# One kernel of token mixing and a quantised layer: the per-step order of all five engines rewritten

## The chip, the core and the metric

One core of one Trainium2 chip. The metric is the device time of one execution in microseconds, here the median of 3 runs; lower is better.

## The reference, cut to what matters

```python
x = x + attn(layernorm(x))            # x: (2, 4096, 512) f32
x = x + ffn(layernorm(x))
# attn, per token: mix = x + xx*time_maa_x;  lo = tanh(mix @ maa_w1.T) @ maa_w2  (4 branches)
#   xm = x + xx*(lo + time_maa)  ->  r, k, v, decay w, gates a, ma, mk, output gate g
# then per head (32 x 32 state s), token after token:
sa = einsum('bhij,bhj->bhi', s, a_)
s = s*w_ + sa*b_ + v_*k_
y = einsum('bhij,bhj->bhi', s, q_)
# y: group norm per head, affine, + bonus, * g, @ Wo.T
# ffn: per row x_q = round(x/x_scale), x_q @ weight_q.T, * x_scale*weight_scale + bias
```

## The kernel before, in words

The 4096 tokens of both sequences are cut into 64 tiles of 64 tokens, so a tile has 128 rows. The recurrence is solved in chunks of 32 tokens (two chunks, c = 0 and 1, in a tile) for 16 heads: within a chunk it is a triangular system, whose inverse is made by squaring (`power` 0, 1, 2, then `half_inverse` and `inverse`), and only the 32 x 32 state passes from chunk to chunk.

The work is a pipeline over tiles. One call of `tile_step(i)` on each engine does four things for four different tiles: **mix** for tile j = i+1 (layer norm, transpose, the four mixed inputs), **project** for tile i (keys, queries, values, gates), **solve** for tile m = i-1 (scores, powers, inverse, the two chunks) and **finish** for tile n = i-2 (group norm, output projection `project_out`, residual, quantisation, `feed_forward`). There are 62 or so full steps, a few partial ones at both ends. The instructions are straight-line code, with no loop on the chip.

Every engine (TensorE `pe`, VectorE `dve`, ScalarE `act`, GpSimd `pool`, SyncE `sp` for the loads and stores) has its own `tile_step`, and the calls in it are the order in which that engine works, written out by hand. Each engine works strictly in that order; between engines there are counting semaphores only: `p_...` is counted up by TensorE, `v_...` by VectorE, `a_...` by ScalarE, `g_...` by GpSimd. A helper such as `quantised(n)` on TensorE waits for `v_q2` (the rows quantised by VectorE), for `v_xm` (VectorE has read the bank that the transpose will overwrite) and then does four transposes.

The names that matter here:
- TensorE: `scores_b`, `scores_k` (64 matmuls each, L1186), `gates` (L1151), `power` (128 matmuls of 32*32, L1208), `half_inverse` (128, L1216), `inverse` (128, L1224), `from_values` (32, L1236), `from_state` (32, L1243), `solve_step` (64, L1252), `from_solutions` (32, L1262), `project_out` (2 matmuls a block, L1272), `transposed_input` (L1103), `low_rank`, `gate_hidden`, `hidden`, `keys`, `queries`, `values` (8 matmuls a block, L1069), `decay_gate`, `output_gate` (L1076), `mixed_inputs` (L1122), `quantised` (L1281), `feed_forward` (L1288). In all 1316 matmuls a step, each with a weight load of its own.
- VectorE: `shift_mix` (xx, then mix, L769), `undecayed` (bt L819, kt L822), `residual` (xres, then its statistics), `update_state` (L900), `decayed_state` (s_old), `quantiser`, `quantised_rows`, `mixed_inputs` (xm_wa and three more, L779), `right_hand_sides` (L896), `decayed` (the two products that make aq).
- ScalarE: `front_transposed` copies the transposed tile to xT; an ACT_TABLE_LOAD is put before a function whose table is not loaded.
- GpSimd: `undecayed` (kmod, kkp, kmod again), `bonus`, `bonus_values` (qkT from rk), `norm2_rstd`, `residual_bias` (x2b), `finish_rows`, `mixed_inputs` (four adds).

## Time and profile before

| | us |
|---|---|
| median of 3 runs | 3234.86 |
| lowest and highest run | 3229.97, 3236.03 |
| profiled execution, span from first to last instruction | 3230.6 |
| TensorE matmuls busy | 3026.2 (94%) |
| TensorE weight loads busy | 2676.0 (83%) |
| VectorE busy | 2659.6 (82%) |
| ScalarE busy | 1987.8 (62%) |
| GpSimd busy | 1252.0 (39%) |
| mean granted clock of TensorE | 0.991 |

Busy time is the union of an engine's instructions; a matmul's end is modelled, so TensorE at 94% is not TensorE at its peak. "issue" in a chain or as releaser is time in which the engine waited for nothing that the profile shows. The profiled execution has no separate time of its own beside its span of 3230.6 us; it lies within the three runs (3229.97 to 3236.03 us).

### The profile page before, as it was taken

To read this page: it belongs to the slowest core of one execution; us is meant where nothing else is said; L and a number is where in the kernel's file an instruction comes from. 1 tells how busy PE (TensorE), PEld (TensorE's weight loads), DVE (VectorE), ACT (ScalarE), POOL (GpSimd) and SP (SyncE) were. 2 spreads that over 40 slices of the span, in tenths; PEclk is the share of its full clock that TensorE was granted. 3 is DMA by queue.
4 is the path that set the end of the run, shared out by engine and by line. 5 is a ranking of instruction groups with operands and counts; after the bars stand their busy time and mean duration, and the time that the engine had idled before them with its cause. 6 is when DMAs were issued, how large, how long until landed. Compare 5 with 4: busy or idle time off the path is not lost.

```text
span 3230.6 us, 182735 instructions
## 1 busy us (share of the span) xinstructions
PE 3026.2 (94%) x84224; PEld 2676.0 (83%) x84224; DVE 2659.6 (82%) x5443; ACT 1987.8 (62%) x3519; POOL 1252.0 (39%) x1161
## 2 busy tenths in 40 slices
PE   5899999999999999999999999999999999999996
PEld 5888888888888888888888888888888888888884
DVE  4687888888888888887888888888888888888885
ACT  3575665665765756756666657567566566566563
POOL 4234334334344344343343343433433433434332
PEclk9999999999999999999999999999999999999998
DMA  3000000000000000000000000000000000000000
GB/s 119 10 23 15 22 20 16 23 20 17 23 20 17 23 20 17 23 20 17 20 18 22 20 17 23 20 17 23 20 17 23 18 18 20 18 22 20 17 17 19
DMA packets 39380, 70.47 MB, mean 22 GB/s; under 512 B 9812, under 2 KB 10836, under 8 KB 38616
## 3 DMA queue, kind: packets, MB, share of 16 engines
q1 hardware_dynamic: 38616, 58.77, 6.7%
q8 instruction: 664, 10.88, 1.4%
q14 instruction: 100, 0.82, 0.1%
HBM read 41.97 MB, written 16.78 MB: 18 GB/s over the span
## 4 chain that ended last, share of the span: by engine, by line
PE 93%; issue 5%; DVE 1%; SPq 1%; ACT 1%; DMA 0%; POOL 0%; POOLq 0%; ACTq 0%; DVEq 0%
PE bank L1069 30%; PE bank_a L1208 12%; PE bank L1272 8%; PE bank_a L1186 4%; PE bank L1076 4%; PE bank_b L1186 4%; PE bank_b L1243 3%; PE bank_b L1236 3%; PE bank_a L1236 3%; PE bank_a L1243 3%; PE bank_a L1216 2%; PE bank_a L1224 2%; PE bank_b L1262 2%; PE bank L1151 2%; PE bank_a L1262 2%
## 5 line engine op out<-in xcount | busy, mean ns | idle before, releaser
L504 ACT ACT_TABLE_LOAD x383 | 491.4, 1283 | 19.3 <-DVE shift L761 12.5
L1069 PE MATMUL bank<-xm_rg,w_r 128*128 128x128 f32 x2048 | 285.4, 282 | 3.5 <-issue 2.7
L1272 PE MATMUL bank<-w_o,yc 128*128 128x512 f32 x512 | 270.8, 630 | 11.1 <-DVE yc L744 9.3
L1208 PE MATMUL bank_a<-pw,w_ffn_int 32*32 32x64 f32 x16384 | 262.0, 215 | 20.1 <-issue 14.9
L1069 PEld LDWEIGHTS bank<-xm_rg,w_r 128*128 128x128 f32 x2048 | 248.9, 191 | 27.9 <-issue 16.9
L1208 PEld LDWEIGHTS bank_a<-pw,w_ffn_int 32*32 32x32 f32 x16384 | 237.4, 105 | 39.4 <-issue 19.0
L1069 PEld LDWEIGHTS bank<-xm_k,w_k 128*128 128x128 f32 x2048 | 241.4, 194 | 12.4 <-issue 3.3
L1069 PE MATMUL bank<-xm_v,w_v 128*128 128x128 f32 x2048 | 249.9, 275 | 1.7 <-DVE kk L744 1.7
L1069 PE MATMUL bank<-xm_k,w_k 128*128 128x128 f32 x2048 | 242.0, 277 | 3.2 <-issue 3.0
L1069 PEld LDWEIGHTS bank<-xm_v,w_v 128*128 128x128 f32 x2048 | 239.2, 192 | 1.8 <-issue 1.8
L504 ACT ACTIVATE u<-bank_b,parity 128x256 f32<-128x256 f32 x128 | 53.7, 470 | 290.8 <-PE bank_b L1252 290.8
L870 DVE STREAM_TRANSPOSE w_ffn_int<-bank_a 128x512 f32<-128x512 f32 x192 | 137.4, 716 | 94.7 <-ACT pw L504 94.4
L399 POOL TENSOR_TENSOR yc<-yc,rkv 128x512 f32<-128x512 f32 x64 | 82.0, 1281 | 327.3 <-ACT yc L504 327.3
L504 ACT ACTIVATE u<-bank_a,parity 128x256 f32<-128x256 f32 x128 | 53.7, 470 | 242.2 <-PE bank_a L1252 242.2
L399 POOL TENSOR_TENSOR xm_wa<-xm_wa,xT 128x512 f32<-128x512 f32 x64 | 75.3, 1177 | 327.9 <-DVE xm_wa L779 327.9
L396 POOL TENSOR_TENSOR kept<-ga,gma 128x512 f32<-128x512 f32 x64 | 81.6, 1274 | 287.1 <-ACT ga L504 287.1
L396 POOL TENSOR_TENSOR kkp<-kk,pinv 128x512 f32<-128x512 f32 x64 | 75.3, 1176 | 288.5 <-DVE kk L744 288.5
L396 POOL TENSOR_TENSOR kmod<-kraw,pinv 128x512 f32<-128x512 f32 x64 | 77.6, 1213 | 258.8 <-ACT pinv L504 258.8
L1208 PE MATMUL bank_a<-first,w_ffn_int 32*32 32x64 f32 x8192 | 134.9, 215 | 26.2 <-issue 25.3
L399 POOL TENSOR_TENSOR o_sb<-o_sb,x2b 128x512 f32<-128x512 f32 x64 | 81.7, 1276 | 200.5 <-DVE o_sb L968 200.5
L396 POOL TENSOR_TENSOR qkT<-qkT,faaaa_T 128x512 f32<-128x512 f32 x64 | 81.5, 1273 | 166.5 <-DVE qkT L914 166.5
L744 DVE TENSOR_TENSOR first<-bank_a,mask_b 128x1024 f32<-128x1024 f32 x64 | 78.4, 1225 | 81.6 <-PE bank_a L1186 81.6
(204 smaller groups left out, 8579.9 us busy)
## 6 DMA issues: line engine op xcount, KB each, us to landing
xin<-in_x SPq DMA_DIRECT2D x128, 128.0 KB, 2.7
xres<-in_x SPq DMA_DIRECT2D x128, 128.0 KB
out<-o_sb SPq DMA_DIRECT2D x128, 128.0 KB, 2.5
w_ffn_int<-in_weight_q SPq DMA_DIRECT2D x1, 2048.0 KB, 9.7
w_k<-in_Wk SPq DMA_DIRECT2D x1, 1024.0 KB
w_r<-in_Wr SPq DMA_DIRECT2D x1, 1024.0 KB
w_v<-in_Wv SPq DMA_DIRECT2D x1, 1024.0 KB
w_o<-in_Wo SPq DMA_DIRECT2D x1, 1024.0 KB, 14.9
```

What stands on the lines that cost most here:

```text
L396: return nc.gpsimd.tensor_tensor(out_, in0, in1, ALU.mult)
L399: return nc.gpsimd.tensor_tensor(out_, in0, in1, ALU.add)
L504: return nc.scalar.activation(out_, in_, func, **kw)
L870: V.transpose(pt, pairs(bank_a)[:, :, 0, :]).then_inc(v_ptT, 1)
L1069: ins = mm(bank[:, o * n:(o + 1) * n], weights[:, k, o * P:(o + 1) * P], x[:, k].rearrange("p b t -> p (b t)"), start=(k == 0), stop=(k == ...
L1076: ins = mm(bank[:, o * TOK:(o + 1) * TOK], weights[:, o * P:(o + 1) * P], hidden[:], start=True, stop=True)
L1186: ins = mm(bank[q, 64 * n:64 * n + 64], both(keys_[q, g]), both(aq[q, g, 0:2]), start=True, stop=True)
L1208: ins = mm(bank_a[q, 64 * n:64 * n + 64], pt[q, g, :], source[q, g, 0:2].rearrange("p j t -> p (j t)"), start=True, stop=True)
L1236: mm(bank[q, 4 * CHUNK * j:4 * CHUNK * j + 3 * CHUNK], both(vT2[q, g]), km[q, g].rearrange("p j t -> p (j t)"), start=(j % 4 == 0), stop=F ...
L1243: ins = mm(bank[q, 4 * CHUNK * j:4 * CHUNK * j + 3 * CHUNK], both(s_old2[q, j]), aq[q, g].rearrange("p j t -> p (j t)"), start=False, stop ...
L1262: ins = mm(bank[q, 4 * CHUNK * j + CHUNK:4 * CHUNK * j + 3 * CHUNK], both(u2[q, j]), first[q, g, 2:4].rearrange("p j t -> p (j t)"), start ...
L1272: ins = mm(fb[0][:], yc[:, k * TOK:(k + 1) * TOK], w_o[:, k, :], start=(k == 0), stop=(k == KB - 1))
```

## The change

The same operations on the same operands. On each engine but SyncE the calls in `tile_step` come in a new order. Three waits are written out that the old order gave by itself (GpSimd `bonus` for `v_k`, GpSimd `residual_bias` for `v_x2`, VectorE `undecayed` for `g_qk`). ScalarE loads its tables by name, four times in a full step.

```diff
@@ -424,6 +424,7 @@
 
             def bonus(m):
                 pool.wait_ge(v_q, count(m, 1, 1))
+                pool.wait_ge(v_k, count(m, 1, 1))
                 mul(qk, aq[:, :, 1, :], kt[:]).then_inc(g_qk, 1)
 
             def weighted_bonus(m):
@@ -451,6 +452,7 @@
                 nc.gpsimd.tensor_tensor(rs2[:, 1:2], rs2[:, 0:1], minus_half[:], ALU.pow).then_inc(g_rs2, 1)
 
             def residual_bias(n):
+                pool.wait_ge(v_x2, count(n, 1, 1))
                 add(x2b[:], xres[:], ffn_bias[:]).then_inc(g_x2b, 1)
 
             def finish_rows(n):
@@ -460,27 +462,26 @@
 
             def tile_step(i, mix=True, project=True, solve=True, finish=True):
                 j, m, n = i + 1, i - 1, i - 2
+                if solve:
+                    bonus(m)
+                    decayed_state(m)
                 if mix:
                     norm_rstd(j)
+                if solve:
+                    weighted_bonus(m)
+                if finish:
+                    add_bonus(n)
                 if project:
                     kept_keys(i)
-                if solve:
-                    decayed_state(m)
-                    bonus(m)
-                if finish:
-                    add_bonus(n)
-                if solve:
-                    weighted_bonus(m)
-                if project:
                     undecayed(i)
+                if finish:
+                    norm2_rstd(n)
                 if solve:
                     bonus_values(m)
-                if finish:
-                    norm2_rstd(n)
+                if mix:
+                    mixed_inputs(j, XWA, XRG)
+                if finish:
                     residual_bias(n)
-                if mix:
-                    mixed_inputs(j, XWA, XRG)
-                if finish:
                     finish_rows(n)
 
             constants()
@@ -639,8 +640,10 @@
                 act.wait_ge(v_ysqT, count(n, 1, 0))
                 run(ysq[:], y_sb[:], ACT.Square).then_inc(a_ysq, 1)
 
-            def exp_tables():
-                nc.scalar.preload_act_table_set("natural_log_exp_and_others")
+            EXP_LN, SIGMOID_TANH = "natural_log_exp_and_others", "sigmoid_and_others"
+
+            def tables(functions):
+                nc.scalar.preload_act_table_set(functions)
 
             def log_variance(n):
                 act.wait_ge(v_yvar, count(n, 1, 1))
@@ -666,62 +669,65 @@
                 j, m, n = i + 1, i - 1, i - 2
                 if solve:
                     removal_pairs(m)
+                if project:
+                    keys(i)
+                if solve:
                     key_pairs(m)
-                if project:
-                    keys(i)
-                if finish:
-                    squared_heads(n)
                 if project:
                     ma_gate(i)
                     a_gate(i)
+                if finish:
+                    squared_heads(n)
+                    tables(EXP_LN)
+                    log_variance(n)
+                if solve:
+                    power(m, 0)
+                if project:
+                    tables(SIGMOID_TANH)
+                    mk_gate(i)
                     squares(i)
-                    mk_gate(i)
-                if solve:
-                    power(m, 0)
-                if finish:
-                    log_variance(n)
+                    decay_gate(i)
+                if finish:
+                    tables(EXP_LN)
                     inverse_deviation(n)
-                if project:
-                    decay_gate(i)
                 if solve:
                     power(m, 1)
+                    value_pairs(m)
+                if project:
+                    log_squares(i)
+                    log_sigmoid(i)
+                    values(i)
                 if finish:
                     head_affine(n)
                 if solve:
-                    value_pairs(m)
-                if project:
-                    log_sigmoid(i)
+                    power(m, 2)
+                if project:
+                    exponentials(i)
+                    key_decay(i)
                 if mix:
                     normalised(j)
-                if solve:
-                    power(m, 2)
-                if project:
-                    values(i)
+                if project:
+                    queries(i)
                 if mix:
                     front_transposed(j)
-                if project:
-                    log_squares(i)
-                    exp_tables()
-                    key_decay(i)
-                    exponentials(i)
+                if solve:
+                    solution(m, 0)
+                if project:
+                    tables(SIGMOID_TANH)
+                    gate_hidden(i)
                 if mix:
                     low_rank(j)
-                if project:
-                    queries(i)
-                if solve:
-                    solution(m, 0)
+                if solve:
                     output_gate(m)
-                if project:
-                    gate_hidden(i)
+                if finish:
+                    quantised(n)
                 if solve:
                     solution(m, 1)
-                if finish:
-                    quantised(n)
+                    outputs(m, 0)
                 if mix:
                     hidden(j, 0)
                     hidden(j, 1)
                 if solve:
-                    outputs(m, 0)
                     outputs(m, 1)
 
             act.wait_ge(const_done, 1)
@@ -819,6 +825,7 @@
                 V.scalar_tensor_tensor(bt[:], by_chunk(ga), -1.0, kkp[:], ALU.add, ALU.mult).then_inc(v_b, 1)
                 dve.wait_ge(g_keep, count(i, 1, 1))
                 dve.wait_ge(g_kz, count(i, 1, 1))
+                dve.wait_ge(g_qk, count(i, 1, 0))
                 V.scalar_tensor_tensor(kt[:], by_chunk(kept), -1.0, kmod[:], ALU.add, ALU.mult).then_inc(v_k, 1)
 
             def decayed(i):
@@ -973,45 +980,46 @@
                 if mix:
                     norm_input(j)
                 if solve:
+                    token_major_values(m)
                     scores_b(m)
+                    enter(m)
                 if finish:
                     head_variance(n)
                 if project:
                     removal_keys(i)
                 if solve:
-                    token_major_values(m)
-                    enter(m)
                     power(m, 0)
+                    token_major_keys(m)
                 if project:
                     key_norm(i)
+                if solve:
+                    scores_k(m)
+                    bonus_rows(m)
+                    power(m, 1)
+                if finish:
+                    head_norm(n)
+                if project:
+                    key_decay(i)
+                if solve:
+                    bonus_sums(m)
+                    power(m, 2)
+                    right_hand_sides(m, 0)
+                if project:
+                    decay_sums(i)
+                if finish:
+                    gate_heads(n)
                 if mix:
                     norm_shift(j)
                 if solve:
-                    token_major_keys(m)
-                if finish:
-                    head_norm(n)
-                if solve:
-                    power(m, 1)
-                    scores_k(m)
-                if finish:
-                    gate_heads(n)
-                if project:
-                    decay_sums(i)
-                if solve:
-                    bonus_rows(m)
-                    power(m, 2)
-                if project:
-                    key_decay(i)
+                    half_inverse(m)
+                if project:
+                    removal_directions(i)
+                if solve:
+                    inverse(m)
                 if mix:
                     shift_mix(j)
-                if solve:
-                    half_inverse(m)
-                    inverse(m)
-                if project:
-                    removal_directions(i)
-                if solve:
-                    right_hand_sides(m, 0)
-                    bonus_sums(m)
+                if project:
+                    undecayed(i)
                 if finish:
                     residual(n)
                 if solve:
@@ -1019,19 +1027,17 @@
                     decayed_state(m)
                 if finish:
                     quantiser(n)
+                    quantised_rows(n)
+                if mix:
+                    mixed_inputs(j, XWA, XWA)
                 if solve:
                     right_hand_sides(m, 1)
-                if finish:
-                    quantised_rows(n)
-                if mix:
-                    mixed_inputs(j, XWA, XWA)
+                if mix:
                     mixed_inputs(j, XK, XV)
                 if solve:
                     bonus(m)
                 if mix:
                     mixed_inputs(j, XRG, XRG)
-                if project:
-                    undecayed(i)
                 if solve:
                     update_state(m, 1)
                 if project:
@@ -1295,66 +1301,68 @@
                     keys(i, [2, 3])
                 if solve:
                     scores_b(m)
+                if project:
+                    gates(i)
+                if solve:
                     scores_k(m)
-                if project:
-                    gates(i)
-                if solve:
                     power(m, 0)
                 if project:
                     queries(i, [0])
+                    decay_gate(i)
                     values(i, [0])
-                    decay_gate(i)
                 if solve:
                     power(m, 1)
                 if project:
-                    queries(i, [1])
                     values(i, [1])
                     values(i, [2])
                     values(i, [3])
-                    queries(i, [2])
+                    queries(i, [1])
                 if solve:
                     power(m, 2)
                     from_values(m, 0)
+                    from_state(m, 0)
+                    half_inverse(m)
+                if project:
+                    queries(i, [2])
+                    queries(i, [3])
+                if finish:
+                    project_out(n, [0])
+                    project_out(n, [1])
+                if solve:
+                    inverse(m)
                 if mix:
                     transposed_input(j)
-                if project:
-                    queries(i, [3])
-                if finish:
-                    project_out(n, [0])
-                if solve:
-                    half_inverse(m)
-                if finish:
-                    project_out(n, [1])
+                if finish:
                     project_out(n, [2])
+                if solve:
+                    solve_step(m, 0)
+                if finish:
+                    project_out(n, [3])
+                if solve:
+                    output_gate(m)
+                    from_solutions(m, 0)
+                if project:
+                    gate_hidden(i)
                 if mix:
                     low_rank(j)
                 if solve:
-                    inverse(m)
-                    from_state(m, 0)
-                if finish:
-                    project_out(n, [3])
-                if solve:
-                    solve_step(m, 0)
-                if project:
-                    gate_hidden(i)
-                if solve:
-                    from_solutions(m, 0)
-                    output_gate(m)
                     from_values(m, 1)
+                if mix:
+                    mixed_inputs(j)
+                if solve:
                     from_state(m, 1)
-                if mix:
-                    mixed_inputs(j)
+                if finish:
+                    quantised(n)
                 if solve:
                     solve_step(m, 1)
                 if finish:
-                    quantised(n)
+                    feed_forward(n)
+                if mix:
+                    hidden(j, 0)
                 if solve:
                     from_solutions(m, 1)
                 if mix:
-                    hidden(j, 0)
                     hidden(j, 1)
-                if finish:
-                    feed_forward(n)
 
             pe.wait_ge(const_done, 1)
             pe.wait_ge(mix_loaded, MIX_LOADED)
```

## Rows read from the trace of the kernel before

**Rows 1.** Windows: 60 full steps; one undisturbed step; one with stalls

```profile
core 0: us, PE busy (x) PEld busy (x) DVE busy (x) ACT busy (x) POOL busy (x), PEclk, DMA share, GB/s
119.80:3070.70 2950.90, 2820.41 (x78962) 2497.42 (x78963) 2487.66 (x5100) 1864.34 (x3301) 1157.23 (x1019) 1.00 0.07 20
...
1743.42:1791.15 47.73, 46.83 (x1316) 41.52 (x1316) 41.74 (x86) 30.98 (x56) 19.27 (x17) 1.00 0.08 20
1546.40:1596.65 50.25, 47.11 (x1316) 41.59 (x1317) 41.44 (x86) 31.19 (x56) 19.27 (x17) 1.00 0.08 20
```

**Rows 2.** Chain that ended last, step from 1743 us: start, us, what

```profile
1763.90 0.59 PE bank L1103 x4
...
1766.24 1.22 PE bank_a L1216 x82
1767.46 1.91 PE bank L1272 x4
...
1770.26 1.19 PE bank_a L1224 x86
...
1773.98 0.68 PE bank_b L1252 x50
...
1775.75 1.09 PE bank_b L1262 x32
1776.84 1.09 PE bank L1076 x8
1777.92 1.47 PE bank_a L1236 x32
1779.39 1.32 PE bank_a L1243 x32
1780.71 1.10 PE bank L1122 x32
...
1782.50 0.68 issue
```

**Rows 3.** Timeline of TensorE, step from 1546 us (pauses inside a group)

```profile
1551.37 1.98 PE L1208 MATMUL bank_a<-first,w_ffn_int 32*32 32x64 f32 x127
1554.52 0.21 PE L1208 MATMUL bank_a<-first,w_ffn_int 32*32 32x64 f32 x1 [1.17 <-issue]
...
1576.85 1.53 PE L1243 MATMUL bank_b<-aq,s_old 64*64 64x96 f32 x31 [0.47 <-issue]
```

**Rows 4.** DMA queues, the page: kind, packets, MB, share of 16 engines

```profile
q8 instruction: 664, 10.88, 1.4%
```

**Rows 5.** Timeline of ScalarE, the copy to xT

```profile
1764.59 0.60 ACT L504 ACTIVATE xT<-bank 128x512 f32<-128x512 f32 x1 [0.70 <-PE bank L1103]
```

**Rows 6.** Timeline of VectorE, the same step

```profile
1765.93 0.69 DVE L744 TENSOR_TENSOR xx<-xT 128x512 f32<-128x512 f32 x1
1766.66 1.14 DVE L769 SCALAR_TENSOR_TENSOR mix<-xx,maa_x,xT 128x128 f32<-128x128 f32 x4
...
1774.13 0.68 DVE L744 TENSOR_TENSOR xres<-bank,xres 128x512 f32<-128x512 f32 x1
...
1776.87 0.45 DVE L900 STREAM_TRANSPOSE state<-bank_b 128x256 f32<-128x256 f32 x1 [0.93 <-PE bank_b L1262]
1777.36 1.74 DVE L744 TENSOR_TENSOR s_old<-state,plast 128x512 f32<-128x512 f32 x1
...
1780.76 0.45 DVE L896 STREAM_TRANSPOSE rhs_sb<-bank_a 128x256 f32<-128x256 f32 x1
...
1781.95 1.12 DVE L779 SCALAR_TENSOR_TENSOR xm_wa<-bank,maa,xx 128x128 f32<-128x128 f32 x4
```

**Rows 7.** The tile kt: VectorE's product, ns min/median/max

```profile
L822 DVE SCALAR_TENSOR_TENSOR kt<-kept,kmod x64: 679/1672/1675, 58.4 to 3159.4; 128x512 f32<-128x512 f32 x64
```

**Rows 8.** Timeline of GpSimd, the same step

```profile
1775.73 1.05 POOL L396 TENSOR_TENSOR qkT<-w_ffn_int,rk 128x512 f32<-128x512 f32 x1
...
1777.25 1.30 POOL L399 TENSOR_TENSOR x2b<-xres,ffn_bias 128x512 f32<-128x512 f32 x1
```

**Rows 9.** Costliest groups, the page: ScalarE's table loads

```profile
L504 ACT ACT_TABLE_LOAD x383 | 491.4, 1283 | 19.3 <-DVE shift L761 12.5
```

20 lines of the change are left out of this document (10 added, 10 removed).

## The prediction

> **What bounds the kernel now.** I read the windows first, for the length of a step and who fills it. Sixty full steps take 2950.9 us, 49.18 us each, and TensorE's matmuls are busy in 2820.4 us of them (96%); VectorE in 84%, ScalarE in 63%, GpSimd in 39% [rows 1]. TensorE's granted clock is 1.00 there, the upper of its two levels (2.4 GHz), and it never pauses long enough to lose it, so the clock is no term. Then the chain that ended last, for what stands between the matmuls. In a step of 47.73 us it is matmuls end to end, and only one pause repeats in step after step: 0.68 us of "issue" in front of `quantised` [rows 2]. `quantised` waits for `v_q2` and for `v_xm`, the second because VectorE must have read bank 1 before the transposes overwrite it; the last part of xm_wa ends at 1781.95 + 1.12 = 1783.07, and the pause at 1782.50 + 0.68 = 1783.18 [rows 2, 6]. So that pause is VectorE being late.
>
> The third view is TensorE's timeline in a longer step (50.25 us with the same 1316 matmuls [rows 1]). There a `power` group of 128 matmuls runs 127, stands still for 1.17 us, and runs the last one; a `from_state` group pauses for 0.47 us in the same way [rows 3]. Nothing in the kernel waits inside a group. The instruction queue shows what it is: 664 packets, 10.88 MB, so 16.4 kB each [rows 4]. TensorE has 2 x 84224 instructions, or 254 a packet: each packet is a block of about 256 instructions, 128 matmuls with their weight loads. The 127 matmuls took from 1551.37 to 1553.35 and the 128th came at 1554.52, so I take it that a block cannot be begun sooner than about 3.2 us after the one before (1554.52 - 1551.37 = 3.15). A `power` group eats one in 2.0 us. A step has 2632 such instructions, 10.3 blocks, so the boundaries wander over the groups and steps differ. The mean step is 49.18 - 47.73 = 1.45 us above the good one, and that one still has a short pause: these stalls cost some 1.5 to 2 us a step. The Trainium skill ("Runtime: NRT & Kernel Launch", Instruction fetch mechanics) says that the refill is 16 KiB blocks of 256 instructions, which the packets agree with, and that fetch is hidden because issue is slower than the fill; by that rule the stall would be nought, and the trace has 1.17 us.
>
> **What TensorE itself gains.** The groups are the same, so its matmul time stays. Tile shapes change about as often as before: `gates` now stands between `scores_b` and `scores_k`, but `from_values` and `from_state` stand together, and so do `gate_hidden` and `low_rank`. I put that at 0, ends -0.2 and +0.2 us a step (a group of 8 matmuls at a change, 1.09 us in `output_gate` [rows 2], carries about 0.2 of it).
>
> **The pause before `quantised`.** In the new order it comes behind `mixed_inputs` and `from_state(1)`, still with both waits. I measure both ways from the start T of `transposed_input`.
> TensorE: `transposed_input` 0.59, block 2 of `project_out` 0.96 (half of 1.91), `solve_step` 0.68, block 3 0.96, `output_gate` 1.09, `from_solutions` 1.09, `gate_hidden` and `low_rank` 2 x 1.09 less the 0.2 of one change, `from_values` 1.47, `mixed_inputs` 1.10, `from_state` 1.32 [rows 2]: 11.2 us.
> VectorE: the copy to xT ends 1.29 after T (1764.59 + 0.60 - 1763.90) [rows 2, 5]; xx and mix 0.69 + 1.14 [rows 6]; bt and kt, which now stand here, 0.68 each if nothing blocks them [rows 7]; then xres to the end of xm_wa. That stretch lasts 1783.07 - 1774.13 = 8.94 before; less the idle 0.93 and the rhs_sb of 0.45 that now comes after, 7.56 [rows 6]. Sum 12.04, and two handoffs of about 0.1: 12.2 us.
> So TensorE waits about 1.0 us where it waited 0.68: **+0.3**.
>
> The uncertain part of the 7.56 is one blocked instruction. kt takes 679 ns once and 1672 at the median, with a GpSimd add beside it [rows 7]; s_old took 1.74 beside x2b [rows 6, 8]. Its unblocked price I estimate from kt's 0.68 (same size, two SBUF inputs), so the block is 1.06. In the new order x2b is later, but `bonus_values` (1.05) starts just when s_old or x2n does, since it is queued behind `norm2_rstd` [rows 8]. I keep one block. Ends: none, and the wait is gone (12.2 - 1.06 is under 11.2), -0.68; a second one, xx behind the last kmod product, +0.5 more, +0.8 in all. The Trainium skill ("SBUF — State Buffer", SBUF: two separate sides) says that VectorE with two SBUF inputs and GpSimd hold a shared port pair exclusively for a whole instruction; the kt row agrees, and it speaks against an order that lays them side by side.
>
> **Behind it.** `feed_forward` now comes after `solve_step(1)`, 1.0 us behind the start of `quantised`; ScalarE must copy qT (0.60 like xT [rows 5]) after the transposes: +0.1. `solve_step(1)` finds its rhs_sb just ready. `hidden(0)` needs GpSimd's add to xm_wa, 1.2 us later, and has 1.9. `keys` has about 0.8 us to spare.
>
> **Instruction blocks.** Before, `power(2)` to `half_inverse` is 2.4 blocks in 7.1 us (2.0 for the power group [rows 3], 1.47, 0.59, some 0.9 for a block of queries, 0.96, 1.22) and `inverse` to `solve_step(0)` 1.8 blocks in 4.3 (1.19, 1.47, 0.96, 0.68) [rows 2]. At 3.2 a block they lack 0.5 and 1.4. After, `power(2)`, `from_values`, `from_state`, `half_inverse` stand together: 2.5 blocks in 6.1, lacking 1.9. `inverse` to `solve_step(0)` lacks 1.5, but that lies after T, where VectorE sets the end and the wait swallows it. So exposed 1.9 before and 1.9 after; I take **+0.1**, with ends -0.3 and +0.6, since how boundaries fall is averaged here.
>
> **ScalarE and the rest.** Six loads a step become four, 2 x 1.283 = 2.6 us less of an engine 63% busy [rows 1, 9]. No pause of TensorE was put down to it: 0. What it would cost if that cover went: a_pw, gate and the u copies have 0.6 to 1 us each before TensorE needs them in the new order. The added waits: `bonus` for `v_k` stands behind `v_q`, which VectorE does later still; `undecayed` for `g_qk` of a tile earlier, long done; `residual_bias` for `v_x2` is issued after the adds, later than the residual. Each 0; behind the last stands `finish_rows`, which needs `v_ffn` later anyway. Loads and stores keep their order, and xres is needed 30 us into a step.
>
> **Sum.** +0.3 +0.1 +0.1 = +0.5 us a step, over 62 steps +31 us. Against the execution's 3230.6 that is 3262; the median of the runs lies 4.3 above it, so **3266 us**.
>
> **Rivals.**
> A, faster: `bonus_values` slips clear of s_old and x2n, VectorE reaches xm_wa by T + 11.2, and the pause of 0.68 goes. That is -0.68 + 0.1 = -0.6 a step, -36: 3199. It decides on one GpSimd instruction of 1.05 us. For it: VectorE's sum without a block is 11.1. Against: nothing else moves that instruction.
> B, a draw: the wait stays what it was, one pause for another: 3235.
> C, much slower: VectorE has no idle time from xx to the next `power(0)`. At the step's end both products of aq now meet GpSimd's xm_rg add and x2b, two blocks of up to 1 us, then vT meets `bonus`; ptT for `power(0)` comes at about the moment TensorE wants it. A microsecond late, or block stalls at their upper end (+0.6), give +1.5 a step: 3328.
> D, the change doesn't do what it says: the table loads stay six. ScalarE has the room; the time is the forecast's.
>
> **How the numbers follow.** The forecast (with D) 0.44, rival A 0.30, B 0.13, C 0.13. The forecast's own ends (wait +0.1 to +0.8, blocks -0.3 to +0.6) go from 3240 to 3300. The range of 8 in 10 takes in A and the lower half of C: 3196 to 3308. A measurement tells 0.2%, 6.5 us or 0.1 us a step, from no change. Faster 0.30, same 0.13, slower 0.57.
>
> **What would show it.** In the changed kernel's chain: about 1 us of "issue" before L1281; s_old or x2n over 1.4 us beside GpSimd's qkT; pauses within the `half_inverse` group, fewer in L1243; four ACT_TABLE_LOADs a step; good steps near 48.0. Wrong would be: no pause before L1281 (A), or a new pause before the first L1208 group or L1186 (C).

## The result and the profile after

The changed kernel takes 3260.99 us (median of 4 runs, 3258.61 to 3263.92), the kernel before 3235.45 on the same chip (4 runs, 3229.97 to 3238.58): a ratio of 1.0081 [1.0067, 1.0096]. The profiled execution spans 3259.1 us, at a mean granted clock of 0.985 (before: 0.991).

The page of the changed kernel: span, engines, the queue that brings instructions, ScalarE's table loads.

```profile
span 3259.1 us, 182613 instructions
...
PE 3046.3 (93%) x84224; PEld 2689.4 (83%) x84224; DVE 2720.8 (83%) x5443; ACT 1756.2 (54%) x3334; POOL 1275.2 (39%) x1161
...
q8 instruction: 664, 10.88, 1.4%
...
L646 ACT ACT_TABLE_LOAD x256 | 328.4, 1283 | 4.6
```

ScalarE's other group of table loads, after and then before:

```profile
L505 ACT ACT_TABLE_LOAD x6 | 7.7, 1283 | 12.3 <-DVE shift L767 12.2
```

```profile
L643 ACT ACT_TABLE_LOAD x64 | 82.1, 1283 | 1.1
```

The same 84224 matmuls and the same 664 blocks of instructions [rows 4]. The table loads are 262 where they were 447: before, the 64 loads by name come on top of the 383 of [rows 9]. That is 4 a step in place of 7, and ScalarE fell from 62% to 54% busy. The time rose all the same. The windows, with the columns of [rows 1], over the same stretch and in one good step:

```profile
119.80:3070.70 2950.90, 2813.01 (x78513) 2486.74 (x78508) 2523.91 (x5051) 1628.03 (x3099) 1168.29 (x1011) 0.99 0.07 20
...
1747.43:1796.20 48.77, 46.90 (x1318) 41.43 (x1316) 42.78 (x87) 27.12 (x52) 19.70 (x17) 1.00 0.08 20
```

In the same 2950.9 us TensorE did 78513 matmuls where it had done 78962 [rows 1], 0.57% fewer. Its chain shows two kinds of pause (start, us, what):

```profile
1748.48 0.45 issue
1748.93 0.38 PE bank L1287 x4
...
1775.20 0.39 PE bank_b L1242 x5
1775.59 0.62 issue
...
1778.90 0.72 PE bank_a L1222 x52
1779.62 0.16 issue
1779.78 0.71 PE bank_a L1222 x46
...
1786.82 0.48 PE bank_b L1258 x38
1787.31 0.63 issue
1787.93 0.39 PE bank_b L1258 x21
```

The first stands before `quantised`, now L1287, and is 0.45 us where it was 0.68 [rows 2]. The others lie within a group, as in [rows 3]: in `from_values`, in `half_inverse`, in `solve_step(0)`. In both kernels a step has 2656 instructions of TensorE, waits included. I cut each of the 61 full steps of both traces into its groups, by counting weight loads, took the time from the first weight load of a group to that of the next, and subtracted the group's own shortest (5th percentile). For the two waits at the step's end I took the time over 0.68, 1.47 and 0.40 us, what their groups take elsewhere. Without these two, the excess is 2.1 us a step before and 2.8 after:

| excess, mean us a step | before | after |
|---|---|---|
| the three `power` | 0.52, 0.28, 0.05 | 0.37, 0.39, 0.14 |
| `half_inverse` | 0.26 | 0.69 |
| queries behind it | - | 0.27 |
| `inverse` | 0.24 | 0.19 |
| `from_state(0)` | 0.34 | 0.05 |
| `solve_step(0)` | 0.09 | 0.38 |
| the rest | 0.32 | 0.37 |
| pause before `quantised` | 0.72 | 0.30 |
| wait for rhs_sb at `solve_step(1)` | - | 0.11 |
| whole step | 49.15 | 49.55 |

The step is 0.40 us longer; times 61 steps that is 24 us, and 25.5 lie between the medians of the runs. Inside the small-tile groups there are 105 pauses of 0.3 us or more before and 116 after, between one weight load and the next. Counted in instructions from the trace's first one, all of them lie at the same place modulo 256, to one instruction; TensorE's 169984 instructions are 664 x 256, one packet for each block. And each of these pauses, in both traces, ends 1.1 to 1.6 us after a packet of the instruction queue has landed. So the in-group pauses are TensorE waiting for its next block.

A part of the excess is not pause but clock. TensorE's granted clock, 0.99 over the whole stretch by the windows, is 0.50, the lower of its two levels (1.2 GHz), in ten short stretches of the full steps after, 38 us together, and in three before, 10 us. All come behind pauses: in nine of the ten one of 1.7 to 2.3 us, in the tenth one of 1.0. Here is one such stretch, and TensorE's timeline ahead of it and in it, after:

```profile
1085.38:1088.79 3.41, 3.41 (x12) 2.38 (x12) 2.33 (x4) 0.70 (x2) 0.97 (x1) 0.50 0.29 77
```

```profile
1083.96 0.44 PE L1222 MATMUL bank_a<-pw,w_ffn_int 32*32 32x32 f32 x28 [1.69 <-issue]
1084.33 2.85 PE L1075 MATMUL bank<-xm_rg,w_r 128*128 128x128 f32 x16
1086.97 2.79 PE L1278 MATMUL bank<-w_o,yc 128*128 128x512 f32 x4
```

In the step from 1747 us the same two groups take 2.05 and 1.88 us. TensorE is busy while the clock is low, so about half of that time is lost, an estimate: 5 us before and 19 after, 0.1 and 0.3 us a step. The row "queries behind it" is mostly that. The median step is even shorter than before, 49.03 us against 49.41; the mean is longer by the few steps with a long pause and a low clock behind it.

The waits (engine line waited for: us in total, times, longest) from 1000 to 2000 us, after, then before, show it in `half_inverse` (L1222; before, L1216) and before `quantised` (L1287; L1281):

```profile
PE bank_a L1222 <- issue: 10.2, 10, 2.3
PE bank L1287 <- issue: 6.1, 13, 0.7
```

```profile
PE bank L1281 <- issue: 12.9, 19, 0.7
...
PE bank_a L1216 <- issue: 3.6, 5, 1.1
```

VectorE's timeline ahead of the end of xm_wa in one step (T, the start of `transposed_input`, is 1785.38), and GpSimd's beside it:

```profile
1786.69 0.69 DVE L750 TENSOR_TENSOR xx<-xT 128x512 f32<-128x512 f32 x1 [0.83 <-ACT xT L505]
...
1791.89 0.69 DVE L750 TENSOR_TENSOR s_old<-state,plast 128x512 f32<-128x512 f32 x1
1792.50 1.27 DVE L959 TENSOR_SCALAR x2n<-xres,mv,rs 128x512 f32<-128x512 f32 x1
...
1795.97 1.13 DVE L785 SCALAR_TENSOR_TENSOR xm_wa<-bank,maa,xx 128x128 f32<-128x128 f32 x4
```

```profile
1791.58 0.55 POOL L452 TENSOR_TENSOR rs<-rs,minus_half 128x1 f32<-128x1 f32 x1 [4.75 <-DVE rs L955]
1792.09 1.40 POOL L396 TENSOR_TENSOR qkT<-w_ffn_int,rk 128x512 f32<-128x512 f32 x1
```

And the three tiles over the whole run (ns, minimum, median, maximum):

```profile
L750 DVE TENSOR_TENSOR s_old<-state,plast x64: 691/691/1556, 103.3 to 3218.8; 128x512 f32<-128x512 f32 x64
```

```profile
L959 DVE TENSOR_SCALAR x2n<-xres,mv,rs x64: 533/1271/1518, 154.2 to 3246.8; 128x512 f32<-128x512 f32 x64
```

```profile
L829 DVE SCALAR_TENSOR_TENSOR kt<-kept,kmod x64: 679/685/689, 51.9 to 3171.0; 128x512 f32<-128x512 f32 x64
```

kt and s_old run free now, against 1672 ns at the median [rows 7] and 1740 in the step shown [rows 6]. x2n is the one that is blocked, beside qkT, which `norm2_rstd` released 0.4 us earlier.

### The profile page after: what moved, and what is told of

Same layout as the page of the kernel before. It is cut to its first block, busy times and chain, and to the rows that moved or that the text cites. A ratio compares the mean times of both kernels' runs of the same rounds, so it can differ in the third digit from the quotient of the medians.

```text
span 3259.1 us, 182613 instructions
## 1 busy us (share of the span) xinstructions
PE 3046.3 (93%) x84224; PEld 2689.4 (83%) x84224; DVE 2720.8 (83%) x5443; ACT 1756.2 (54%) x3334; POOL 1275.2 (39%) x1161
## 4 chain that ended last, share of the span: by engine, by line
PE 93%; issue 5%; DVE 1%; ACT 1%; POOL 0%; POOLq 0%; ACTq 0%; DVEq 0%
PE bank L1075 30%; PE bank_a L1214 12%; PE bank L1278 7%; PE bank_a L1192 4%; PE bank_b L1192 4%; PE bank L1082 4%; PE bank_b L1242 3%; PE bank_a L1249 3%; PE bank_a L1242 3%; PE bank_b L1249 3%; PE bank_a L1222 3%; PE bank_a L1230 2%; PE bank L1128 2%; PE bank L1157 2%; PE bank_a L1268 2%
## 5 line engine op out<-in xcount | busy, mean ns | idle before, releaser
L1075 PE MATMUL bank<-xm_v,w_v 128*128 128x128 f32 x2048 | 258.2, 279 | 2.8 <-issue 2.8
L505 ACT ACTIVATE qT<-bank 128x512 bf16<-128x512 bf16 x64 | 38.2, 597 | 264.0 <-PE bank L1287 264.0
L452 POOL TENSOR_TENSOR rs<-rs,minus_half 128x1 f32<-128x1 f32 x64 | 35.0, 548 | 354.2 <-DVE rs L955 354.2
L505 ACT ACTIVATE pw<-bank_a 128x512 f32<-128x512 f32 x192 | 113.4, 590 | 103.7 <-PE bank_a L1214 103.7
L505 ACT ACTIVATE pinv<-cum 128x512 f32<-128x512 f32 x64 | 40.4, 631 | 230.8 <-DVE cum L797 230.8
L396 POOL TENSOR_TENSOR s_old<-state,plast 128x512 f32<-128x512 f32 x64 | 67.6, 1057 | 184.7 <-DVE plast L750 184.7
L1192 PE MATMUL bank_a<-aq,w_ffn_int 64*64 64x64 f32 x4096 | 134.4, 221 | 2.2 <-ACT w_ffn_int L505 2.2
```

Of the source, the lines that this page charges most:

```text
L396: return nc.gpsimd.tensor_tensor(out_, in0, in1, ALU.mult)
L505: return nc.scalar.activation(out_, in_, func, **kw)
L1075: ins = mm(bank[:, o * n:(o + 1) * n], weights[:, k, o * P:(o + 1) * P], x[:, k].rearrange("p b t -> p (b t)"), start=(k == 0), stop=(k == ...
L1192: ins = mm(bank[q, 64 * n:64 * n + 64], both(keys_[q, g]), both(aq[q, g, 0:2]), start=True, stop=True)
```

## The experiments

My theory after the result: the new clustering of small matmuls (`from_state(0)` and `half_inverse` behind `power(2)`) costs block stalls (pauses at the boundary of an instruction block), and x2n blocked beside qkT costs the pause. The rivals: table loads, or some unseen wait. The excesses below are worked out as in the table above, over all full steps.

**half_late**, on the changed kernel: `half_inverse` moved behind one block of queries.

```diff
                     from_state(m, 0)
-                    half_inverse(m)
                 if project:
                     queries(i, [2])
+                if solve:
+                    half_inverse(m)
+                if project:
                     queries(i, [3])
```

> The changed kernel with one call moved on TensorE: half_inverse(m) goes behind queries(i, [2]), so that 8 slow matmuls (0.9 us) stand between from_state and the 128 fast ones. Block theory (256 instructions come no sooner than about 3.2 us after the block before): power(2), from_values, from_state, half_inverse are 2.5 blocks in 6.1 us now and lack 1.9 us; spread out they lack about 1. Averaged over where boundaries fall that is 0.25 to 0.4 us a step, so 15 to 25 us less: 3236 to 3246. Rival (the pauses in L1222 and around are waits for other engines, or the longer step comes from VectorE alone): the group waits as long wherever it stands, within 5 us of 3261.

Measured: 3249.42 us, before 3227.35 on that chip, 1.0068 [1.0043, 1.0093]. That can't be told from the changed kernel's 1.0081: 4 us by the ratios where 15 to 25 were expected, so the time is the rival's. The excess of `half_inverse` and the queries fell from 0.96 to 0.35 us, as looked for, but `inverse` rose from 0.19 to 0.41 and `solve_step(0)` from 0.38 to 0.53. More than half of the stalls moved on.

**values_early**, on the changed kernel: GpSimd does `bonus_values(m)` ahead of `undecayed(i)` instead of behind `norm2_rstd(n)`.

```diff
                     kept_keys(i)
+                if solve:
+                    bonus_values(m)
+                if project:
                     undecayed(i)
                 if finish:
                     norm2_rstd(n)
-                if solve:
-                    bonus_values(m)
```

> The changed kernel with one call moved on GpSimd: bonus_values(m) goes ahead of undecayed(i). Theory of the blocked instruction (x2n takes 1.27 us at the median and 0.53 alone, because GpSimd's qkT product stands beside it, and TensorE waits for the end of that VectorE chain before the transposes of quantised): x2n falls to about 0.53, the pause before those transposes (about 0.5 us at the mean) is gone, 0.3 to 0.5 us a step, 18 to 30 us less: 3231 to 3243. Rival (the extra time is all in TensorE's instruction blocks): x2n falls as well, but the time stays within 5 us of 3261, since stalls elsewhere take the place of the pause.

Measured: 3239.20, 1.0033 [1.0019, 1.0048]. x2n ran free:

```profile
L960 DVE TENSOR_SCALAR x2n<-xres,mv,rs x64: 534/541/1501, 152.1 to 3221.3; 128x512 f32<-128x512 f32 x64
```

The pause before `quantised` is gone in all 61 full steps; 0.28 us at `solve_step(1)`, for rhs_sb, took a part of its place. The mean step fell from 49.55 to 49.19. So one blocked instruction was worth 0.5% of the time, some 15 us, a little under the 18 to 30 expected. A part of that can be the clock: this trace has four stretches at the lower level in its full steps, not ten. What is left, +0.3%, is the block stalls less what the step's end saves.

**both**: the two edits together.

```diff
# GpSimd: bonus_values(m) ahead of undecayed(i)
# TensorE: half_inverse(m) behind queries(i, [2])
```

> Both moves together: half_inverse(m) behind queries(i, [2]) on TensorE, and bonus_values(m) ahead of undecayed(i) on GpSimd. If the two causes are separate, the gains add up: 33 to 55 us less than the changed kernel, 3206 to 3228, which is below the kernel before (3235). If only blocks count it is as fast as the first move alone, if only the blocked instruction counts as the second alone.

Measured: 3242.66, 1.0049 [1.0030, 1.0068]: no better than values_early alone. The gains were expected to add up to less than the kernel before, and did not: with the pause gone too, moving `half_inverse` gains nothing that can be measured.

**auto_tables**, on the changed kernel: no loads by name, so a load is put before a function whose table isn't there.

```diff
             def tables(functions):
-                nc.scalar.preload_act_table_set(functions)
+                pass
```

> The changed kernel without its named table loads, so that they are placed automatically: about two more ACT_TABLE_LOADs of 1.283 us a step, six again. My prediction's view (ScalarE is not what TensorE waits for): within 6 us of the changed kernel, 3255 to 3267. Rival (the new order lives by the four loads, its margins on ScalarE are used up): 2.6 us a step come through in part, 3300 or more.

Measured: 3252.11, 1.0083 [1.0053, 1.0113].

```profile
L505 ACT ACT_TABLE_LOAD x383 | 491.4, 1283 | 19.0 <-DVE shift L767 12.3
```

That is 121 loads more than in the changed kernel, 155 us of ScalarE, and the ratios of the two can't be told apart: their intervals overlap, and the wider is 0.3% to either side. The loads by name are worth nothing here that these runs can measure, and cost nothing.

**pad_48 and pad_128**, on the changed kernel: `inverse` repeats 80 of its matmuls, which brings a step from 2656 to 2816 instructions, 11 blocks of 256 to the instruction. Each boundary then lies at the same instruction of every step. The two differ only in where: the first `low_rank` of the run repeats 24 or 64 matmuls, 48 or 128 instructions, once.

```diff
             def low_rank(i):
                 pe.wait_ge(v_mix, count(i, 1, 1))
+                for _ in range(3 if i == 0 else 0):   # pad_128: 8
+                    full(fb[3], w_maa1, mix, [0])
 ...
-                for n, g, q in ALL:
+                for n, g, q in ALL[:40] + ALL:
```

> The changed kernel with its TensorE program lengthened: inverse does its first 40 products twice (80 more small matmuls of the same result, 160 instructions, some 0.75 us a step), so that a step has 2816 instructions, exactly 11 blocks of 256, and every block boundary falls at the same place in every step; and low_rank of the first tile is done 3 times more, 48 instructions, which sets that place. Block theory, with 3.2 us a block: boundaries at this place leave 1.8 us lacking a step, against 2.9 measured in the changed kernel, so with the 0.75 of added work it is within 30 us of the changed kernel's time, 3240 to 3300, and all full steps are of one length within 0.5 us. Rival (the pauses are waits for other engines): about 3310, and steps go on differing by 3 us and more.

> The same, but low_rank of the first tile is done 8 times more: 128 instructions instead of 48, so that all block boundaries lie 80 instructions further back in every step. Block theory: 4.0 us lacking a step at this place, a part of it behind transposed_input and swallowed by the wait there, so 1.5 to 2.3 us a step more than the run with 48, 90 to 140 us: about 3340 to 3430. Rival: the five added repeats cost 5 us at the start and nothing else.

Measured: pad_48 3338.12, 1.0344 [1.0325, 1.0363]; pad_128 3515.24, 1.0893 [1.0867, 1.0920]. Five repeated blocks of eight matmuls, once in the whole run, made a difference of 177 us. The chain of pad_48, then of pad_128:

```profile
1758.90 1.22 PE bank_a L1224 x82
...
1761.65 0.40 issue
...
1764.38 1.23 PE bank_a L1232 x82
1765.60 0.39 issue
```

```profile
1752.69 0.98 PE bank_a L1224 x68
1753.67 1.69 issue
...
1761.07 1.84 PE bank_a L1232 x125
1762.91 2.26 issue
```

In pad_128 the boundary falls near the end of `half_inverse` (L1224) in each step; TensorE's timeline has the same 28 matmuls behind it 55.5 us later:

```profile
1755.36 0.58 PE L1224 MATMUL bank_a<-pw,w_ffn_int 32*32 32x32 f32 x28 [1.69 <-issue]
...
1810.86 0.44 PE L1224 MATMUL bank_a<-pw,w_ffn_int 32*32 32x32 f32 x28 [1.96 <-issue]
```

Mean steps are 50.63 and 53.39 us. The 80 matmuls themselves are about 0.74 (80 of 1.19/128 us), so against the changed kernel's 49.55 pad_48 pays 0.3 more for its boundaries and pad_128 3.1. I had looked for a difference of 90 to 140 us and for pad_48 at 3240 to 3300: both too low. Direction and mechanism hold. A good half of the 177 us is the granted clock: in its full steps pad_128 has 198 us at the lower level and pad_48 14, so by half of that time, an estimate, 92 us of the difference; the mean clock fell to 0.961 over the run (pad_48: 0.989). The steps were to be of one length within 0.5 us, and are not: 49.65 to 52.50 us in pad_48, 51.30 to 55.85 in pad_128. The place of the boundaries is fixed in every step, the length of the pauses at them is not.

**bias_last**, on the kernel before: GpSimd's x2b (`residual_bias`) goes behind `mixed_inputs(j)`, so that s_old is not blocked.

```diff
             def residual_bias(n):
+                pool.wait_ge(v_x2, count(n, 1, 1))
+                pool.wait_ge(v_ffn, count(n, 1, 1))
 ...
                     norm2_rstd(n)
-                    residual_bias(n)
                 if mix:
                     mixed_inputs(j, XWA, XRG)
                 if finish:
+                    residual_bias(n)
                     finish_rows(n)
```

> The kernel before with one call moved on GpSimd: residual_bias(n) goes behind mixed_inputs(j) and waits for v_ffn, so that x2b no longer stands beside VectorE's s_old (1.44 us at the median, 0.69 alone). Theory of the blocked instruction: s_old falls to 0.69, VectorE's chain to xm_wa is 0.75 shorter, and the pause of 0.68 to 0.72 us before the transposes of quantised, the only one that was not an instruction block, is gone in every step: 0.6 to 0.7 us a step, 37 to 43 us less than the kernel before, ratio 0.987 to 0.989, faster than both kernels. Rival (that pause is bound by something else in VectorE's chain, or given back elsewhere): ratio over 0.995.

Measured: 3227.47 against 3227.06, 1.0003 [0.9993, 1.0012]. s_old is free in all 64 steps, and the pause before `quantised` (here L1283) stays at 0.68. Its tile row, VectorE's timeline and the chain:

```profile
L746 DVE TENSOR_TENSOR s_old<-state,plast x64: 691/691/693, 103.5 to 3181.0; 128x512 f32<-128x512 f32 x64
```

```profile
1769.52 0.45 DVE L898 STREAM_TRANSPOSE rhs_sb<-bank_a 128x256 f32<-128x256 f32 x1 [1.15 <-PE bank_a L1245]
...
1770.71 1.12 DVE L781 SCALAR_TENSOR_TENSOR xm_wa<-bank,maa,xx 128x128 f32<-128x128 f32 x4
```

```profile
1769.47 1.10 PE bank L1124 x32
1770.57 0.68 PE bank_a L1254 x50
1771.26 0.68 issue
1771.94 0.38 PE bank L1283 x4
```

The expected 0.987 to 0.989 did not come; this is the rival's result. VectorE gained a microsecond in this step and then stood idle 1.15 us for TensorE's `from_state(1)` (L1245), because `right_hand_sides(1)` came ahead of `quantised_rows`. From the end of that group VectorE had rhs_sb, the rows and xm_wa to do, 2.4 us, while TensorE had 1.10 + 0.68 = 1.78. By these rows the order alone makes a pause of 0.6; the next run tests it.

**tail** takes that order apart, on the kernel before: bias_last, and the end of the step in the changed kernel's manner. **tail_bias_old** is the same without bias_last.

```diff
# VectorE
                     quantiser(n)
-                    right_hand_sides(m, 1)
                     quantised_rows(n)
                     mixed_inputs(j, XWA, XWA)
+                    right_hand_sides(m, 1)
# TensorE
                     from_values(m, 1)
-                    from_state(m, 1)
                     mixed_inputs(j)
-                    solve_step(m, 1)
+                    from_state(m, 1)
                     quantised(n)
-                    from_solutions(m, 1)
+                    solve_step(m, 1)
+                    feed_forward(n)
                     hidden(j, 0)
+                    from_solutions(m, 1)
                     hidden(j, 1)
-                    feed_forward(n)
# ScalarE: quantised(n) ahead of solution(m, 1)
```

> The kernel before with x2b moved as in bias_last, and the end of the step alone in the manner of the new order: TensorE does mixed_inputs(j) ahead of from_state(m, 1), then quantised, solve_step, feed_forward, hidden(0), from_solutions, hidden(1); VectorE does quantised_rows and xm_wa ahead of right_hand_sides(m, 1); ScalarE copies qT ahead of the u copies. New theory for the pause before the transposes: VectorE first waits for TensorE's from_state(1) (1.15 us idle before rhs_sb in bias_last, although s_old was 0.69), then does rhs_sb, the quantised rows and xm_wa, 2.4 us, while TensorE has 1.8 us of work; the order itself makes the 0.72. With rhs_sb behind xm_wa the pause goes: 0.6 to 0.7 us a step, ratio to the kernel before 0.986 to 0.990, and the places where instruction blocks lack stay as in the kernel before. Rival (the pause is a cost of switching to the bf16 transposes, or comes back as another wait): ratio over 0.996.

> The same end of the step, but with x2b where it was, beside s_old. Now nothing of TensorE's stands ahead of VectorE's chain, so the block of s_old (1.4 us in place of 0.69) should reach TensorE: VectorE's chain from the end of from_solutions(0) is 4.9 us and 0.75 more, TensorE has 5.1, so a pause of about 0.5 us stands before the transposes: ratio 0.994 to 0.998. Rival (GpSimd's block is covered here too): as fast as the run tail, within 0.2%.

Measured: tail 3209.55 against 3230.38, 0.9934 [0.9917, 0.9951], faster than both kernels, though not by the 0.986 to 0.990 expected. tail_bias_old 3223.07, 0.9981 [0.9969, 0.9994], at the edge of the expected 0.994 to 0.998. The windows of tail, what its `solve_step(1)` still waits for, and s_old in tail_bias_old:

```profile
119.80:3070.70 2950.90, 2846.42 (x79681) 2512.09 (x79677) 2478.98 (x5138) 1884.56 (x3335) 1170.05 (x1026) 1.00 0.08 20
```

```profile
PE bank_a L1254 <- DVE rhs_sb L898: 18.9, 60, 0.3
```

```profile
L744 DVE TENSOR_TENSOR s_old<-state,plast x64: 691/1352/1741, 102.9 to 3182.9; 128x512 f32<-128x512 f32 x64
```

79681 matmuls in the stretch against 78962 [rows 1], 0.9% more. The pause of 0.72 is gone and a wait of 0.28 us for rhs_sb is new. That makes 0.44 us a step, 27 us over 61 steps, with nothing of TensorE changed in the middle of the step; 21 were measured, and the interval is 16 to 27. With this order the block of s_old counts, 0.5% between the two kernels, and its pause before `quantised` is back, 0.44 us a step; with the old order it counted nothing.

**cluster**, on tail: `from_state(0)` and `half_inverse` directly behind `from_values(0)`, as in the changed kernel. **cluster2** mends what cluster got wrong.

```diff
                     from_values(m, 0)
+                    from_state(m, 0)        # cluster2: these two behind transposed_input(j)
+                    half_inverse(m)
                 if mix:
                     transposed_input(j)
# both: blocks 0, 1 and 2 of project_out together; cluster2: VectorE's right_hand_sides(m, 0) ahead of half_inverse
```

> The run tail with one thing of the new order added on TensorE: from_state(m, 0) and half_inverse(m) go straight behind from_values(m, 0), so that power(2), from_values, from_state and half_inverse stand together as in the changed kernel. Same instructions, same 2656 a step, no other engine touched. Block theory: these 320 matmuls are 2.5 blocks in 6.1 us, so more boundaries come too early: 0.6 us a step more than tail in stalls at boundaries (summed from the durations of the groups at 3.2 to 3.4 us a block), some 30 to 45 us: ratio to the kernel before 1.003 to 1.008, which is most of the way back to the changed kernel. The pauses should lie inside half_inverse. Rival (density of small matmuls doesn't matter, only waits): within 0.2% of tail, 0.9934.

> The run cluster also waited before solve_step(0), because transposed_input had moved behind the cluster and VectorE's shift_mix stands ahead of its inverse; so it did not test the density alone. Here transposed_input stays where it is in tail, from_state(m, 0) and half_inverse(m) come straight behind it, inverse(m) stands behind low_rank as before, and on VectorE right_hand_sides(m, 0) moves ahead of half_inverse so that solve_step(0) finds its rhs_sb. Block theory: at 3.2 to 3.4 us a block the boundaries lack 0.6 to 0.7 us a step more than in tail, none of it from waits: 35 to 45 us, ratio to the kernel before 1.004 to 1.008. Rival (only waits count, and cluster's loss was its wait before solve_step(0)): within 0.2% of tail, 0.9934.

Measured: cluster 3336.78 against 3229.37, 1.0329 [1.0306, 1.0353]; cluster2 3253.93 against 3238.64, 1.0046 [1.0031, 1.0061]. Expected was 1.003 to 1.008, and cluster can't be read as a price of stalls. Its `transposed_input` comes late, VectorE's `shift_mix` stands ahead of the inverse and waits for it, and `solve_step(0)` pays; its waits from 1000 to 2000 us:

```profile
DVE xx L746 <- ACT xT L506: 48.6, 20, 4.4
...
PE bank_b L1254 <- DVE rhs_sb L898: 23.0, 18, 1.3
```

That wait is 1.3 us a step. The clock adds to it: 25 stretches at the lower level, 99 us together, where tail has one.

cluster2 has no such wait and stands 1.1% above tail by their ratios (1.0046 and 0.9934). Its excess in `half_inverse` is 0.56 us a step against 0.28 in tail, and in `solve_step(0)` 0.45 against 0.07 (some of it waits of the weight loads for VectorE's copy of the inverse). `from_state(0)` has 0.30 less and `inverse` 0.26 less. In all the groups' excess is 2.3 us a step against 2.0. But cluster2 also has 0.65 us of pause before `quantised` that tail lacks. So the clustering costs some 0.3 us of stalls net, and more than half of the 1.1% is a wait: this run does not show the stalls alone either.

The whole new order of TensorE alone, with the other engines as they were, and the reverse, are orders in which, as I read the waits, engines wait for each other for ever; they were not tried.

## Why the prediction was right, and where its terms were not

3266 was forecast and 3261 measured, +1.0% and +0.8%, in the range and on its side. That the number fits so well is luck: two terms of the sum were wrong and cancelled, and a third, the clock, was put at nothing and was not.

**The pause before `quantised`: +0.3 forecast, -0.4 measured** (-0.3 with the wait that took a part of its place). It was to grow from 0.68 to 1.0 and fell from 0.72 to a mean of 0.30, 0.41 with the wait for rhs_sb behind it. TensorE's path was right: 11.2 us worked out, 11.18 in the trace without stalls. VectorE's was too long: xm_wa ends at 1795.97 + 1.13 = 1797.10, which is T + 11.72, not T + 12.2. The step that failed is the price of a block, 1.06, taken from kt. x2n took 1.27 us where it takes 0.53 alone, so its block cost 0.74; it had begun 0.4 us into qkT, not at its start, which may be why (the rows don't show where within x2n the wait lies). The two handoffs of 0.1 were not there either. That one block is there, and which instruction it hits, was right: values_early took it away and 0.5% went with it. That is also what rival A described, and it would have come true with one GpSimd call elsewhere, though at 1.0033, not at A's 0.989, since A took the stalls at +0.1.

**What the wait swallows: all forecast, a quarter measured.** I let the stalls between `inverse` and `solve_step(0)` cost nothing, since VectorE sets the end behind them. In the 35 full steps without a stall in `solve_step(0)` the pause before `quantised` is 0.48 to 0.72 us. In the other 26 the stall is 0.33 to 1.64 us, 0.9 on average; the pause is all but gone, and 0.28 us at `solve_step(1)` comes instead. So a stall of 0.9 takes off about 0.2: the pause can give no more than its own half microsecond, and the wait for rhs_sb takes 0.28 of that back.

**Instruction blocks: +0.1 forecast, +0.75 measured**, beyond the upper end of +0.6. Of this some 0.2 is the low clock behind the pauses, so the pauses alone are about +0.5. The mechanism was right (the pads: 177 us by the place of the boundaries alone, clock included) and so was the cluster, whose lack I put at 1.9 us of 2.5 blocks. Wrong was the reading that "exposed 1.9 before and 1.9 after" gives the same price. After, `half_inverse` and the queries behind it pay 0.96 where `half_inverse` paid 0.26. Wrong, too, was the one spacing of 3.2 us on which both sums rest. It came from a single row. The blocks that begin with a pause inside a small-tile group begin 1.9 to 5.3 us after the block before them in the trace of before, 60 of 105 later than 3.5, and 2.5 to 5.9 after, 75 of 116 later than 3.5. What is steady is the 1.1 to 1.6 us from the landing of the packet. What decides when the packet is fetched stays open. half_late shows that such a stall moves in good part to the next small group when one group is moved.

**The clock, put at nothing.** "It never pauses long enough to lose it" was wrong for the kernel before already: [rows 1] shows 1.00 because it rounds a mean. The clock is 0.50 in three stretches of the full steps before, behind pauses of 1.1 to 1.7 us, and in ten after. By half of their time that is +0.2 us a step, an estimate.

**What bounds the kernel before.** The reading of [rows 2, 6], that VectorE is late at `quantised`, holds. That the 1.74 us of s_old were a part of that was not written as a cause, but I priced the new order as though VectorE's busy time from xres on were all one chain. bias_last shows that it was not: VectorE idled 1.15 us for TensorE in the middle of it. The pause came of `right_hand_sides(1)` ahead of the rows.

**Behind it, +0.1:** the size is right and the place is not. `feed_forward` shows no pause in the trace; the 0.11, counted above already, is `solve_step(1)` waiting for rhs_sb, which I had just ready.

**ScalarE, 0:** right, though before it was seven loads a step and not six: the forecast counted [rows 9] and left out the load by name. auto_tables has six, and its time can't be told from the changed kernel's. Rival D fell (four loads a step), and would have made no difference that these runs can measure.

**Added waits and shape changes, 0:** the shortest steps of both kernels, without pauses, sum to 46.3 us a step, so the change of shapes is 0 as put. No added wait shows up among the waits. Rival C did not come: no pause before the first `power` group or the scores beyond the block stalls.

**The ends.** With the wait at +0.1 to +0.8 and the blocks at -0.3 to +0.6 the sum goes from 3229 to 3328, and not from 3240 to 3300, if both ends fall together; the latter had no reason beside it.

**What was to show it.** Four table loads a step, x2n blocked beside qkT (up to 1518 ns), more pauses in `half_inverse` (35 of over 0.15 us against 16) and fewer in `from_state(0)` (10 against 20) are there. The pause of about 1 us before L1287 is not: it is 0.48 in most of the steps that have it.

## What to carry to other kernels

Before an order of engines is rewritten, follow the late operand back through its engine until that engine idles: the instruction that blocks (s_old) is worth nothing while there is slack behind it, the order that makes the slack (rhs_sb ahead of the rows) is worth 0.2% by itself, and the two together 0.7%. Long runs of small matmuls pay for instructions as well as for arithmetic, and moving one group moves much of the stall to the next small one. A slack swallows no more than its own length, and a long pause is paid twice where the granted clock falls behind it. A forecast that comes out right as a sum should still be checked term by term.

## What was not expected of the hardware

The place of the block boundaries alone is worth 5% (pad_48 against pad_128: 3338 and 3515 us for the same steps), a good half of it by the lower clock behind the pauses. Single pauses in the chain are up to 2.26 us. The Trainium skill ("Runtime: NRT & Kernel Launch", Instruction fetch mechanics) calls the crossing of a boundary mostly hidden. In these runs pauses and clock together cost 2.1 us of every 49.15 us before and 2.8 of 49.55 after, so the measurement decides against the sentence for such groups.

TensorE's granted clock was 0.961 in pad_128 and 0.977 in cluster, against 0.985 to 0.992 in all the other profiled runs. In the full steps that is 198 and 99 us at the lower level, against 3 to 38 in the others, and every such stretch comes close behind one or two pauses. That pauses of one to two microseconds cost clock as well had no place in my expectation. Not every long pause does: of the 14 over 1.5 us in the changed kernel's full steps, five have no such stretch behind them, and why is left open.

x2n, a product with one 128x512 input and two columns of scalars, was blocked by GpSimd as products of two tiles are: 1271 ns at the median and up to 1518, against 533. The Trainium skill ("SBUF — State Buffer", SBUF: two separate sides) names two ways in which a VectorE instruction takes the shared pair, two SBUF inputs or a 2-port performance mode; which of them x2n met is left open here.
